# A macaron block (MoE, attention, MoE) on one core: the order of the attention batches on VectorE, three steps moved to Pool, one expert register per slot

## The reference

```
x = x + 0.5 * ffn(layernorm(x))
x = x + attention(layernorm(x))        # 16 heads of 8, rotary q and k, softmax, w_o
x = x + 0.5 * ffn(layernorm(x))

ffn(x):
    logits = x @ Wg + bg               # 8 experts
    top2_vals, top2_idx = top_k(logits, 2)
    scores = softmax(top2_vals)
    y_e = gelu(x @ W1[e] + b1[e]) @ W2[e] + b2[e]      # hidden 512
    out = sum over the two chosen e of score * y_e
    return layer_norm(x + out) * gamma + beta
```

## Time and profile before

| | |
|---|---|
| runs | 501.21, 501.49, 502.33 us, median 501.49 |
| profiled execution | 504.88 us, of which span 503.1 |
| PE busy | 409.7 us, 81% |
| DVE busy | 354.2 us, 70% |
| ACT busy | 257.1 us, 51% |
| POOL busy | 210.8 us, 42% |
| blocks of phase 0 | about 54 to 175 us of the span |
| attention batches | about 182 to 350 |
| blocks of phase 1 | about 352 to 478 |

### The profile page before, as it was taken

The page is one execution under the profiler, slowest core; times in us unless marked ns, Lnnn a source line. Parts: engine busy times, 40 slices in busy tenths (PEclk is TensorE's granted clock), DMA queues, the critical chain, the costliest instruction groups (busy, mean ns, idle before and its releaser), DMA issues. The chain is left out here.

```text
span 503.1 us, 10245 instructions
## 1 busy us (share of the span) xinstructions
PE 409.7 (81%) x3224; PEld 331.3 (66%) x3224; DVE 354.2 (70%) x1148; ACT 257.1 (51%) x515; POOL 210.8 (42%) x268
## 2 busy tenths in 40 slices
PE   1542699999999987989898999998999699999810
PEld 1441488887798865666575767666598588888700
DVE  4798345547776758999999999785177644567846
ACT  2531257655556453756566575665555345555500
POOL 5478755474444302120323243143057637344521
PEclk9999999999999998999999898999699889999975
DMA  9613711113110017960000000001012211133131
GB/s 269 252 47 76 220 38 48 54 49 96 42 43 27 29 48 247 314 199 22 20 14 7 18 12 13 12 22 46 20 47 60 64 38 47 49 91 96 59 99 42
DMA packets 32691, 37.71 MB, mean 75 GB/s; under 512 B 4992, under 2 KB 27520, under 8 KB 32240
## 3 DMA queue, kind: packets, MB, share of 16 engines
q1 hardware_dynamic: 27632, 27.32, 18.3%
q0 software_dynamic: 4544, 9.35, 5.7%
q10 hardware_dynamic: 464, 0.38, 0.4%
HBM read 26.64 MB, written 20.36 MB: 93 GB/s over the span
## 5 line engine op out<-in xcount | busy, mean ns | idle before, releaser
L1189 ACT ACTIVATE stage<-ps 128x512 f32<-128x512 f32 x78 | 46.6, 597 | 89.8 <-PE ps L726 89.6
L1761 DVE TENSOR_REDUCE mx<-ps 128x4 f32<-128x1024 f32 x64 | 77.1, 1213 | 9.0 <-PE ps L840 9.0
L1651 DVE TENSOR_TENSOR ring_hi<-ps,ring_hi 128x512 fp32r<-128x512 f32 x78 | 53.8, 690 | 34.2 <-ACT ring_hi L1196 34.1
L1243 ACT ACTIVATE stage<-ps 128x1024 f32<-128x1024 f32 x64 | 65.4, 1022 | 24.0 <-PE ps L851 23.2
L749 PE MATMUL ps<-w_hl,ring_hi 128*128 x234 | 65.2, 347 | 0.8 <-DVE stage L1659 0.8
L1645 DVE TENSOR_TENSOR bx<-ps,bx 128x128 fp32r<-128x128 f32 x78 | 22.4, 287 | 61.3 <-ACT bx L1171 60.1
L499 POOL DMA_INDIRECT expert_y<-stage x39 | 38.9, 997 | 56.8 <-DVE stage L1659 56.4
L750 PE MATMUL ps<-w_hl,ring_hi 128*128 x312 | 61.0, 236 | 0.0
L499 POOL DMA_INDIRECT expert_y<-stage,arena x39 | 38.8, 995 | 50.7 <-DVE stage L1659 45.1
L480 POOL DMA_INDIRECT sorted_x<-rows,place_at x32 | 32.7, 1023 | 58.6 <-DVE place_at L1477 50.5
L750 PEld LDWEIGHTS ps<-w_hl,ring_hi 128*128 128x128 f32 x312 | 54.5, 193 | 0.0
(11 more groups left out here) (197 smaller groups left out, 1045.4 us busy)
## 6 DMA issues: line engine op xcount, KB each, us to landing
sorted_x<-fill SPq DMA_DIRECT2D x8, 1096.5 KB, 16.9
stage<-w SPq DMA_DIRECT2D x16, 256.0 KB, 6.7
y_got<-expert_y SPq DMA_DIRECT2D x24, 128.0 KB, 2.5
stage<-sorted_x SPq DMA_DIRECT2D x39, 64.5 KB, 1.9
arena<-sorted_x SPq DMA_DIRECT2D x39, 64.5 KB, 1.8
x_tok<-x SPq DMA_DIRECT2D x4, 256.0 KB, 5.3
sorted_x<-rows,place_at POOLq DMA_INDIRECT x64, 2.4
stage<-sel SPq DMA_DIRECT2D x1, 1024.0 KB, 5.9
```

Source lines behind the costliest of these rows:

```text
L1189: act.activation(g_full[:, s, :], ps[:, H_BANK, :], ACT.Gelu).then_inc(g_done, 1)
L1243: act.activation(prob[:, 2 * v:2 * v + 2, :], ps[:, at:at + 2, :], ACT.Exp, scale=SCALE)\
L1651: vec.tensor_tensor(bg_lo[:, s, :, :].rearrange("p c n -> p (c n)"), ps[:, G_BANK, :], bg_hi[:, s, :, :].rearrange("p c n -> p (c n)").bit ...
L1761: vec.tensor_reduce(mx[:, t, :].rearrange("p (r g j) -> p r j g", r=2, g=2)[:, pair, 2 * jp:2 * jp + 2, :], ps[:, at:at + 2, :].rearrange( ...
```

## The change

It replaces `load_experts` by `load_expert`, one register per slot (four in rotation), slots 0 and 1 ahead of the loop and slot s + 2 after `down` of iteration s. The wait for the second part of the table comes with the load of slot 9 or 13, so in iteration 7 or 11. On VectorE, in batches 1 to 5: in those with `norm`, the sum of `combine` stands between maxima 0 and 1, its apply behind the second `divide`, the statistics of `a_norm` before maxima 4; `gating` and `add_chosen` come last in the batch, so that maxima 6 and 7 follow the rotation. In `gating` the subtraction of the top two comes after the members. `a_norm`'s normalisation of batch b + 3 and `pre_apply` go to Pool, and so does the sum of the rotation; VectorE makes the rounded value by an add of its own. TensorE gets one more `scores_owned` with two filler matmuls before `qk_swapped` in batches from 1 on.

```diff
@@ Pool, new and changed
+            def att_apply(b):
+                gp.wait_ge(att_norm[2], 2 * b + 2)
+                gp.wait_ge(a_xt_filled, b)
+                for t in range(BT):
+                    op = gp.tensor_scalar(xn[:, t, :], x_tok[:, b * BT + t, :], mv[:, t, 0:1], rstd[:, t:t + 1],
+                                          ALU.subtract, ALU.mult)
+                op.then_inc(a_ln_done, 1)
+
+            def pre_apply(u):
+                first, many = unit_tiles(u)
+                gp.wait_ge(rstd_ready, 2 * u + 2)
+                for c in range(first, first + many):
+                    op = gp.tensor_scalar(rows1[:, c, 0:D], x_tok[:, c, :], fmv[:, c, 0:1], frstd[:, c:c + 1],
+                                          ALU.subtract, ALU.mult)
+                op.then_inc(ln_done, 1)
@@ low_rotated
+                gp.wait_ge(sin_done, b + 1)
+                if b:
+                    gp.wait_ge(rot_ready, b)
+                gp.tensor_tensor(rot, t_cos, t_sin, ALU.add).then_inc(rot_sum, 1)
+                gp.wait_ge(rot_sum, b + 1)
                 gp.wait_ge(rot_hi_done, b + 1)
@@ batch of Pool
+                if b >= 1 and norm:
+                    post_rstd_of(b + 3)
+                    att_rstd(b + 3)
+                    att_apply(b + 3)
                 if b >= 2:
                     second_ids(PAIRS + b - 2)
...
                 if more:
                     low_rotated(b + 2, p)
-                if norm:
+                if b >= 1:
+                    pre_apply(FIRST_UNIT + b - 1)
+                if b == 0:
                     post_rstd_of(b + 3)
                     att_rstd(b + 3)
+                    att_apply(b + 3)
@@ blocks, TensorE
-                def load_experts(i):
...
+                def load_expert(i):
                     if i == 0:
                         pe.wait_ge(sched_ready, TABLES * phase + 1)
                     if i == EARLY[phase]:
                         pe.wait_ge(sched_ready, TABLES * phase + 2)
+                    pe.load(expert_regs[i % 4], expert_of[0:1, i:i + 1])
+                    experts[i] = pe.snap(expert_regs[i % 4], min_val=0, max_val=EXPERTS - 1)
...
-                    if s + 1 < SLOTS and s + 1 == slot_group(phase, s + 1)[0]:
-                        load_experts(s + 1)
...
                         down(n0 + s - 2, experts[s - 2])
+                    if s + 2 < SLOTS:
+                        load_expert(s + 2)
@@ batch of TensorE
                 if project_next:
+                    if b:
+                        scores_owned(b + 1, 6)
+                        keep_busy(2 * (6 % MAX_BUF), 2)
                     qk_swapped(b + 2, p)
@@ rotate_cos, rotate_sin, VectorE
                 vec.wait_ge(qk_filled, b + 1)
+                if b:
+                    vec.wait_ge(rot_sum, b)
+                    vec.wait_ge(rot_hi_done, b)
...
                 vec.wait_ge(sin_done, b + 1)
-                if not (isinstance(b, int) and b == 0):
-                    vec.wait_ge(rot_ready, b)
-                vec.tensor_tensor(rot, t_cos, t_sin, ALU.add).then_inc(rot_sum, 1)
-                vec.wait_ge(rot_sum, b + 1)
-                vec.tensor_copy(rot_hi[:, p, :, :], rot).then_inc(rot_hi_done, 1)
+                vec.tensor_tensor(rot_hi[:, p, :, :], t_cos, t_sin, ALU.add).then_inc(rot_hi_done, 1)
@@ batch of VectorE (late = 1 <= b < BATCH - 2)
                 if place_next:
                     maxima(b + 1, 0)
+                if late and norm:
+                    combine(b + 3, apply_part=False)
+                if b and place_next:
+                    maxima(b + 1, 1)
...
                     divide(b - 1, 1)
+                if late and norm:
+                    combine(b + 3, sum_part=False)
...
                     placing(FIRST_UNIT + b - 3)
+                if late and norm:
+                    vec.wait_ge(x_done, b + 4)
+                    a_norm(b + 3, apply_part=False)
                 if place_next:
                     maxima(b + 1, 4)
...
                     rotate_sin(b + 2, p)
-                if b >= 2:
-                    gating(FIRST_UNIT + b - 2)
-                    add_chosen(FIRST_UNIT + b - 2)
-                if norm:
+                if b == 0:
                     combine(b + 3, apply_part=False)
+                if b >= 2 and not late:
+                    gating(u)
+                    add_chosen(u)
                 if place_next:
                     maxima(b + 1, 6)
...
                     maxima(b + 1, 7)
                     negate(b + 1, 1)
-                if norm:
-                    a_norm(b + 3, stats_part=False)
-                if tail:
-                    pre_apply(FIRST_UNIT + b - 1)
+                if b >= 2 and late:
+                    gating(u)
+                    add_chosen(u)
```

More of the change, by code:

```diff
@@ L619, in _ @@
         def _(pe):
-            expert_regs = [pe.alloc_register(f"pe_expert{i}") for i in range(12)]
+            expert_regs = [pe.alloc_register(f"pe_expert{i}") for i in range(4)]
             def pass3(out_ap, wh, wl, vh, vl, start=True, stop=True):
@@ L758, in blocks @@
                 n0 = phase * SLOTS
-                experts, loaded = {}, []
-                def load_experts(i):
-                    many = slot_group(phase, i)[1]
-                    third = 4 * (len(loaded) % 3)
+                experts = {}
+                def load_expert(i):
                     if i == 0:
@@ L768, in load_experts @@
                         pe.wait_ge(sched_ready, TABLES * phase + 2)
[L769 to L774, removed]
+                    pe.load(expert_regs[i % 4], expert_of[0:1, i:i + 1])
+                    experts[i] = pe.snap(expert_regs[i % 4], min_val=0, max_val=EXPERTS - 1)
+                load_expert(0)
+                load_expert(1)
                 for s in range(SLOTS + 2):
@@ L1431, in gating @@
                 vec.wait_ge(gate_steps, at.now())
-                vec.tensor_tensor(gap[:, first:first + many], top[:, 0:many, 1], top[:, 0:many, 0], ALU.subtract)\
-                    .then_inc(gap_ready, 1)
                 for t in range(many):
@@ L1446, in gating @@
                                   picks[:, u % 2, 1, 0:many, :], ALU.add).then_inc(members_set, 1)
+                vec.tensor_tensor(gap[:, first:first + many], top[:, 0:many, 1], top[:, 0:many, 0], ALU.subtract)\
+                    .then_inc(gap_ready, 1)
             def add_chosen(u):
@@ L1793, in batch @@
             def batch(b, p, tail=True, place_next=True, project_next=True, norm=True):
+                u = FIRST_UNIT + b - 2
+                late = 1 <= b < BATCH - 2
                 if place_next:
                     maxima(b + 1, 0)
-                if place_next:
+                if b == 0:
                     maxima(b + 1, 1)
-                if b == 0:
                     combine(2, apply_part=False)
+                if late and norm:
+                    combine(b + 3, apply_part=False)
+                if b and place_next:
+                    maxima(b + 1, 1)
                 if tail:
@@ L1827, in batch @@
                 if b >= 2:
-                    logits_of(FIRST_UNIT + b - 2)
+                    logits_of(u)
                 if tail:
```

1 line of the change is left out of this document (removed).

## The result

The changed kernel took 514.03 us (median; 512.04 to 516.93), the kernel before 501.91 beside it: ratio 1.022, interval 1.013 to 1.031. On another chip of the study it was 1.017 (1.009 to 1.025). 509.5 was forecast, 502 to 515.5 the range. The time lies inside it, and the reasons don't hold as they stand: term A had the wrong sign, and something that I hadn't priced cost more than all that I had put on A. The profiled execution took 512.04, span 510.2, so it is 7.1 longer in span than that of before.

The account below looks back on a forecast made before the run. VectorE was taken to set the pace in attention batches, TensorE in the blocks. Median 501.5 + 8.4 (expert loads) - 0.3 (batch loop) = 509.6, stated as 509.5 us, range 502 to 515.5.

Parts of the forecast that it names:

- term A: Expert registers: 78 single loads for 22 group loads, exposed before `up`'s weights, slots 2.91 instead of 2.55; sum +8.4 us.
- loads hidden: Rival: without group loads the sequencer's lead at L719 exceeds 0.46 in most slots; time 494; chance 0.09.
- Term B: Attention batches: two normalisations, the cast and the subtraction's contention leave VectorE, 2.4 of 23.1 us, leaving 20.7.
- Term C: Attention batches: the new order makes a loop through the cosine product; batches 2 to 5 22.1, 22.7, 22.7, 21.2; sum -0.3.
- Pool: Pool takes two applies (0.59 each) and a sum (1.28); cost nothing, up to 1 per batch in three batches.
- Pool or the clock: Rival: rot_ready late on Pool, or TensorE's clock falling after idling before qk_swapped; 513 to 516; chance 0.14.

Follow-up runs that it names:

- the loads alone: The kernel before with single-register `load_expert` in the place of `load_experts`: ratio 0.985 (0.979 to 0.991), 6.1 us faster.
- ids first: The changed kernel with `second_ids` ahead of the attention-norm steps of batch b+3 on Pool: ratio to before 0.987, on another chip 1.000.

## Why the prediction was right in its number and wrong in its reasons

**Term A** is the step that failed: "It is ahead by 0.13. That is all the cover." I took the time between the sequencer's event at L719 and the weight load for all the time that the sequencer can lose. The rows that I didn't look at are the ones ahead of that event. In the kernel before, one slot on, the last register operation of `down` is at 419.0 and the next event at 419.5:

```profile
L750 PEldq FUSED_REGOPS  x1: 46/46/46, 419.0 to 419.0; - x1
...
L719 PEldq EVENT_SEMAPHORE  x1: 51/51/51, 419.5 to 419.5; - x1
```

In these 0.5 us the profile shows no register operation and no event. A load of 0.30 with its move fits, and in the changed kernel it does: the last register operation is at 425.2, the load at 425.3, the event at 425.8, and `up`'s first weight load comes 0.11 after `down`'s last as before. My reading, which no row shows, is that the sequencer stood there with a full queue. My sign of being wrong, slots that stay at 2.5, is what came. What the groups cost was sized rightly (0.52 in every slot with one; slots of 3.07 are gone), so the bound that I named for free loads, -7, is nearly what the loads alone gave, -6. The rival "loads hidden" had the right sign, and its condition (a lead over 0.46 at L719) was as wrong as the forecast's: the lead there is still about 0.1.

**Term B** was right in kind: the normalisations and the cast left VectorE, the subtraction fell from 1.19 to 0.16, VectorE's busy time in a batch from 22.3 to 19.9, the 2.4 forecast. Pool's prices were low: an apply takes 0.79 and not 0.59, and the sum 1.78 beside VectorE's add (ns min/median/max). With ids first the sum comes after that add in batches 3 and 4 and takes the 1.27 that I had:

```profile
L512 POOL TENSOR_TENSOR arena<-arena x8: 1282/1779/1785, 146.7 to 327.4; 128x512 f32<-128x512 f32 x8
...
L462 POOL TENSOR_SCALAR x_t<-x_tok,mv,rstd x10: 783/798/833, 207.6 to 298.2; 128x128 f32<-128x128 f32 x10
```

What the subtraction gave up came back in part in the cast before it, in the kernels that keep gating behind the rotation. In the changed kernel gating stands after maxima 7, out of its reach. In the earlier trace rows I gave VectorE half or two thirds of the blocks; it is half in both stretches, two thirds are ScalarE's. No sum used it.

**Term C** was right where it could be seen, with ids first: 21.9, 22.8, 22.8, 21.7 for 22.1, 22.7, 22.7, 21.2. From the first maximum to the end of the cosine product it is 13.7 in batch 3 (252.57 to 266.23), where I had 13.9; the wait before qk_swapped is 0.8, not 1 to 3. Batch 5 was 0.5 longer than its own steps had summed to. Batch 1 lost 4.9 and not 3.3: besides the rotation TensorE waits there for a maximum (1.0) and for the attention's low part on VectorE (1.8), both behind the combine that was put ahead of them, and it ran at the lower clock after them (a first matmul of 0.47). Over batches 1 to 5 that gives +1.1 where I had -0.3.

**Pool** is the part with the missing step. I had listed that the attention norm moves ahead on Pool, and asked only whether rot_ready would be late. It moved past `second_ids` as well, which ScalarE waits for ahead of the exponentials of step 4, and in Pool's new order it waits itself for VectorE's statistics in mid-batch. VectorE's order (statistics later than the ids are needed) is harmless without Pool's (norm first), as ids first shows; together they tie step 5 to the statistics. Pool's order with VectorE's old one wasn't run. Three rows of VectorE's timeline in batch 4 show its side: the subtraction of the top two, now 0.16; the cosine product; and the rotation's rounded sum 5.6 us behind that, with a maximum and the sine product (1.9 together) as the only work between.

```profile
285.04 0.16 DVE L1473 TENSOR_TENSOR gap<-top 128x2 f32<-128x2 f32 x1
...
298.45 0.66 DVE L1772 TENSOR_TENSOR arena<-ps,rope_sb 128x512 f32<-128x512 f32 x1
...
304.72 0.69 DVE L1781 TENSOR_TENSOR x_hi<-arena 128x512 fp32r<-128x512 f32 x1
```

The 0.3 of cover that I gave the placing matmuls was gone as well: they wait 0.5 for Pool with ids first. And the sum on Pool, which I gave up to 0.3 in batch 0, costs 1.5 in slot 33 of phase 0 (5.2 in all kernels that have it, 3.7 in all that don't), through a wait of the next cosine product that I didn't list.

So, in the times: -6 for the loads, +8 to +11 for the stall, and for everything else what is left of +12, 7 to 10. The traces place 3.8 of it: the 1.5 of slot 33, and 2.3 in batches 1 to 5 (115.0 us with ids first, 112.7 with the loads alone). On one chip that last term was +1 (0.987 against 0.985 for the loads alone). Where ids first gave 1.000 the loads alone weren't run, but the kernel with loads, moved subtraction and `pre_apply` on Pool was, at 495.1, 8.5 below ids first; its batches 1 to 5 are 3.7 shorter than those of the loads alone, which leaves some 5 (an estimate). So its size stays open. My +8.4 and -0.3 come near the sum by chance. The rival "Pool or the clock" is the nearest of the four, with another release on Pool than the one named in it.

## What to carry to other kernels

When a step is moved ahead in one engine's list, go through every semaphore that the steps behind it set, and ask for each what stands behind its waiter on the waiter's engine: a copy of 0.2 us held TensorE for 3.4. For what a sequencer can hide, look back from an instruction to the last one that the sequencer could have issued earlier, not forward to when the engine takes it. When an engine at its limit gets work taken away, its order is the next bound: with VectorE's busy time at 21.0 us a batch and not 22.3, the last half microsecond moved gave nothing, and two maxima in a better place gave 0.5 in batch 4.

## What the runs showed of the hardware

A register load of one took 295 ns at least, 300 in the median and 490 at most over all 78 places of the table (the longest in any run was 687), two registers took 530 and four some 1000, so no part of the table was dear to read. The contention between Pool and VectorE isn't tied to an instruction: the subtraction's 1.0 us went to a cast of four elements a lane (0.17 to 0.79), which has one input and ended with Pool's operation. TensorE after idling 0.76 to 0.80 before qk_swapped kept the full clock in some batches and fell to the lower one in others, in the same kernel; after 3.43 it fell at once in batches 3 and 4 of the changed kernel. Without the filler it fell at once after 1.43 in batch 3, and in batch 4, after 1.44, it stayed full for another 1.2 us and then fell. And chips differ: the kernel before took 502 to 504 on three and 521 to 522 on two. The kernel with ids first, profiled on one of each, took 4 us longer in slot 3 of phase 0, some 7 longer in slots 8 to 10 of phase 1 and 4.6 longer between batch 6 and phase 1 on the slower chip, and as long in the slots at TensorE's pace; what it waited for there is open.
